# Float32 scores and output projection on TensorE: from 64x128 tiles to 64x64 tiles

## The chip, the cores and the metric

The kernel runs on one core of one Trainium2 chip. The metric is the time of one execution in device microseconds. TensorE (PE) multiplies, VectorE (DVE), ScalarE (ACT) and GpSimd (POOL) do the elementwise work, and SyncE (SP) issues the DMAs. The engines run their own programs and meet at semaphores.

## The reference

32 sequences of 256 rows with 128 channels go through a feed-forward block, an attention block and the same feed-forward block again:

```
x = x + 0.5 * ffn(layernorm(x))
x = x + attn(layernorm(x))       # linear attention: 16 heads of 8, states multiplied over K=2
x = x + 0.5 * ffn(layernorm(x))
```

The feed-forward block is a softmax attention of 16 heads of width 64, with mixtures of 8 experts at its values and at its output:

```
q, k   = x Wq[h], x Wk[h]                       # 16 heads, width 64
v      = sum_e mix[t,h,e] * (x Wv[e])           # mix: sigmoid of the two largest gates
scores = softmax(q k^T / 8)                     # 256 x 256 per head
res    = sum_h sum_e mask[t,h,e] * (attn[t,h] Wo[e])
```

All of it is float32.

## The kernel before

**Passes and quarters.** A pass is one feed-forward block of one sequence. There are 64: 7 first blocks to start with, then second and first blocks in turn (25 of each), then 7 second blocks. A pass has four quarters of four heads each, so that there are 256 quarters that attend; `n` counts quarters, and `p, r = divmod(n, 4)`. All engines run over the same quarters in a software pipeline written out by hand: in quarter n TensorE computes the scores of quarter n, the product of probabilities and values of quarter n-1, the projections q and k of quarter n+1, and transposes the probabilities of quarter n. Other passes' steps are put in at fixed quarters: the mixed values of pass p+1 at r = 2 and 3 (`values`), the output of pass p-2 at r = 1 (`output`), the expansion of the masked attention at r = 2 (`expand`), and the steps of the attention block of passes p-2 to p-4 where these were first blocks. Since first and second blocks alternate, so do two kinds of pass: I call a pass *even* where p-2 and p-4 were first blocks (passes 26 and 24, for instance, are first blocks, so pass 26 is even), and *odd* where p-3 was one.

**TensorE's order in a quarter**: scores (L373), then values (L385) at r = 2 and 3 or output (L399) at r = 1, product (L415), expand (L427) at r = 2, the projections (L432 to L434, called through `split_mm`), small steps, and 16 transposes (L453, `turn`). Each transpose group of four waits until its PSUM bank is vacant. Four banks go round in the order of the work, so that a turn waits for whatever used the bank four items before.

**Tiles of the array.** A matmul whose operands lie on 64 partitions uses half of the array's rows; one whose output has 64 partitions uses half of its columns. The trace writes rows*columns: scores and output are 64*128 (two tiles, picked by the head or by the half of the rows), values 64*64 (four tiles), product and expand 128*64 (two tiles), projections and transposes 128*128. One float32 matmul of the kernel appears as two MATMUL instructions with a weight load (PEld) each.

**Who waits for scores.** DVE takes the maxima of each pair of heads (L595), ACT takes the exponentials (L700) and then copies the next q and k from PSUM (L738). The other DVE work of a quarter follows the copy of the product (L619, which waits for the product): at r = 0 RSUM and MASKR (L598, L602, ahead of that copy), the choice of experts (`EQ`, `FW`, `MAXR`, `F`, L555 to L565) and, at r = 3, MIX (L654), which SP writes to memory and reads back as MT. POOL builds from it BT for the values (L804), and MB for expand (L810); at r = 2 of an odd pass it first normalises AA (L792 to L797) from DVE's statistics (L572, L575). At r = 2, XT is copied by ACT (L763) and DVE (L669).

Of the kernel before, what the change touches and what calls it, by code (L numbers as in the profile page):

```python
# [12 lines left out]
P = 128  # L13
# [9 lines left out]
def macaron_kernel(nc, x, WqT, WkT, WvT, WgT, WoT, aWq, aWkv, aWo, b_q, b_kv, b_o, ln_g, ln_b,  # L23
                   ident_d, diagv_d, diago_d, ramp_d, heads_d, out):
    NSEQ, T, C = x.shape
    NT = T // P
    E, DH = WoT.shape[1], WoT.shape[0]
# [6 lines left out]
    with ctx:  # L34
        def sb(name, shape, dtype=F32):
            return ctx.enter_context(nc.sbuf_tensor(name, shape, dtype))
# [18 lines left out]
        wo = sb("wo", [P, E, C])  # L55
# [17 lines left out]
        QK = sb("QK", [P, 2, 2, T])  # L73
# [33 lines left out]
        OT = sb("OT", [P, E, P])  # L107
# [17 lines left out]
        psS = ctx.enter_context(nc.psum_tensor("psS", [P, 2, 2, NT, T], F32))  # L125
# [97 lines left out]
        def bank(*item):  # L223
            return psT[:, place[item] % BANKS, :]
# [5 lines left out]
        def wait_freed(eng, *item):  # L230
            if item in place:
                eng.wait_ge(s_free[place[item] % BANKS], place[item] // BANKS + 1)

        def wait_vacant(eng, *item):

            if place[item] >= BANKS:
                eng.wait_ge(s_free[place[item] % BANKS], place[item] // BANKS)

        def full(*item):
            return s_full[place[item] % BANKS]  # L240
# [124 lines left out]
        def tensor_program(eng):  # L365
            def scores(n, ab):
                wait_freed(eng, "qk", 2 * n + ab)
                if n >= 1:
                    eng.wait_ge(s_exp, 8 * (n - 1) + 4 * ab + 4)
                for it in range(NT):  # L370
                    for j in range(2):
                        own = slice(64 * j, 64 * j + 64)
                        last = eng.matmul(psS[:, ab, j, it, :], QK[own, ab, 0, it * P:(it + 1) * P], QK[own, ab, 1, :], start=True, stop=True)  # L373
                last.then_inc(s_score)

            def values(q, half):
# [14 lines left out]
            def output(q):  # L391
                for i in range(2):
                    wait_vacant(eng, "output", q, i)
                    wait_freed(eng, "expand", q, i)
                eng.wait_ge(s_late, 16 * 14)
                for e in range(E):
                    for i in range(NT):
                        rows = slice(64 * i, 64 * i + 64)
                        last = eng.matmul(bank("output", q, i)[:, 0:C], OT[rows, e, :], wo[rows, e, :], start=e == 0, stop=e == E - 1)  # L399
                        if e == E - 1:  # L400
                            last.then_inc(full("output", q, i))

            def product(m):
                pm, r = divmod(m, 4)
# [26 lines left out]
            def split_mm(dst, left, right):  # L431
                eng.matmul(dst, left(0), right(0), start=True, stop=False)  # L432
                eng.matmul(dst, left(0), right(1), start=False, stop=False)  # L433
                return eng.matmul(dst, left(1), right(0), start=False, stop=True)  # L434
# [25 lines left out]
            for n in QUARTERS:  # L460
                p, r = divmod(n, 4)
                if works(n):
                    scores(n, 0)
                    scores(n, 1)
# [4 lines left out]
                if r == 1 and runs(p - 2):  # L469
                    output(p - 2)  # L470
# [8 lines left out]
                if r in (0, 1) and runs(p + 2):  # L479
                    q = p + 2  # L480
                    wait_vacant(eng, "expert", q, r)
                    split_mm(bank("expert", q, r), lambda c: XT[:, q % 3, c, r * P:(r + 1) * P], lambda c: wv[:, c, :]).then_inc(full("expert", q, r))
                if r == 0 and attends(p - 3):
                    q = p - 3
# [4 lines left out]
                    for k in range(2):  # L489
                        for t in range(NT):  # L490
                            last = eng.matmul(M[:, k * C:(k + 1) * C], KV[:, t, k * C:(k + 1) * C], KV[:, t, (2 + k) * C:(3 + k) * C],
                                              start=t == 0, stop=t == NT - 1)
# [3 lines left out]
                if r == 0 and attends(p - 4):  # L496
                    q = p - 4
# [5 lines left out]
                if r == 1 and attends(p - 3):  # L503
                    q = p - 3
# [6 lines left out]
                if r == 2 and runs(p + 3):  # L511
                    q = p + 3
# [4 lines left out]
                if r == 2 and attends(p - 2):  # L517
                    q = p - 2
# [3 lines left out]
                if r == 3 and runs(p + 3):  # L522
                    q = p + 3
# [4 lines left out]
                    for it in range(NT):  # L528
                        last = split_mm(M[:, it * T:(it + 1) * T], lambda c: XT[:, q % 3, c, it * P:(it + 1) * P], lambda c: wg[:, c, :])
                    last.then_inc(full("gates", q))  # L530
                if r == 3 and attends(p - 3):
                    q = p - 3
# [3 lines left out]
                if r == 3 and attends(p - 2):  # L536
                    q = p - 2
# [349 lines left out]
```

## Time and profile before

| | us |
|---|---|
| median of 3 runs | 2708.53 (2707.15 to 2710.92) |
| the profiled execution, its own time | 2715.99 |
| its span | 2714.2 |
| PE busy | 2599.0 (96%) |
| PE weight loads busy | 2310.9 (85%) |
| DVE, ACT, POOL busy | 2056.0, 1882.0, 967.4 |
| mean granted TensorE clock, share of full | 0.994 |

The ends of matmuls are modelled, and a matmul is shown longer than the time after which the next starts. So the distance between the starts of two phases says more than the busy share.

### The profile page before, as it was taken

To read this page: it belongs to the slowest core of one execution; us is meant where nothing else is said; L and a number is where in the kernel's file an instruction comes from. 1 tells how busy PE (TensorE), PEld (TensorE's weight loads), DVE (VectorE), ACT (ScalarE), POOL (GpSimd) and SP (SyncE) were. 2 spreads that over 40 slices of the span, in tenths; PEclk is the share of its full clock that TensorE was granted. 3 is DMA by queue.
4 is the path that set the end of the run, shared out by engine and by line. 5 is a ranking of instruction groups with operands and counts; after the bars stand their busy time and mean duration, and the time that the engine had idled before them with its cause. 6 is when DMAs were issued, how large, how long until landed. Compare 5 with 4: busy or idle time off the path is not lost.

```text
span 2714.2 us, 106002 instructions
## 1 busy us (share of the span) xinstructions
PE 2599.0 (96%) x43712; PEld 2310.9 (85%) x43712; DVE 2056.0 (76%) x3370; ACT 1882.0 (69%) x5957; POOL 967.4 (36%) x805
## 2 busy tenths in 40 slices
PE   4999999999999999999999999999999999999998
PEld 3888888888888888888888888888888888888897
DVE  5777777777777777777777777877777777777763
ACT  3767767677767677677777676776776766677675
POOL 2243433423424334334234243343342433433321
PEclk8999999999999999999999999999999999999998
DMA  4545445555454554555554545545555545454553
GB/s 123 158 137 144 142 134 146 140 149 148 138 153 139 139 149 144 150 142 144 149 148 138 153 135 143 147 141 153 138 144 147 148 134 145 135 155 138 145 154 101
DMA packets 519180, 387.23 MB, mean 143 GB/s; under 512 B 213936, under 2 KB 436016, under 8 KB 510512
## 3 DMA queue, kind: packets, MB, share of 16 engines
q1 hardware_dynamic: 518272, 379.60, 50.3%
q8 instruction: 352, 5.77, 0.9%
q14 instruction: 124, 1.02, 0.1%
q10 hardware_dynamic: 432, 0.85, 0.1%
HBM read 191.64 MB, written 188.74 MB: 140 GB/s over the span
## 4 chain that ended last, share of the span: by engine, by line
PE 72%; DVE 14%; ACT 8%; issue 5%; POOL 1%; DMA 0%; SPq 0%; ACTq 0%; DVEq 0%; POOLq 0%
PE psS L373 16%; PE psT L453 15%; PE psT L415 14%; PE psT L432 5%; ACT PB L700 5%; PE psT L399 4%; PE psT L434 4%; PE psT L433 4%; DVE NMAX L595 4%; PE psT L385 4%; DVE FW L559 3%; PE psT L542 2%; PE psT L427 2%; DVE EQ L555 2%; DVE AO L619 1%
## 5 line engine op out<-in xcount | busy, mean ns | idle before, releaser
L700 ACT ACTIVATE PB<-psS,NMAX 128x256 f32<-128x256 f32 x2048 | 943.5, 488 | 590.8 <-DVE NMAX L595 590.8
L595 DVE TENSOR_REDUCE NMAX<-psS 128x4 f32<-128x1024 f32 x512 | 603.1, 1220 | 102.3 <-PE psS L373 102.3
L453 PE MATMUL psT<-ident,PB 128*128 128x128 f32 x4096 | 521.5, 277 | 59.8 <-DVE XT L669 37.3
L453 PEld LDWEIGHTS psT<-ident,PB 128*128 128x128 f32 x4096 | 451.8, 141 | 127.2 <-DVE XT L669 53.3
L415 PE MATMUL psT<-V,PT 128*64 128x64 f32 x16384 | 538.2, 224 | 2.7 <-issue 2.6
L415 PEld LDWEIGHTS psT<-V,PT 128*64 128x64 f32 x16384 | 501.9, 138 | 42.1 <-issue 25.8
L373 PE MATMUL psS<-QK 64*128 64x256 f32 x4096 | 511.8, 389 | 0.0
L804 POOL TENSOR_TENSOR BT<-MT,diagv 128x1024 f32<-128x1024 f32 x128 | 320.2, 2502 | 481.4 <-DMA MT<-MIXd 481.4
L680 DVE COPY PT<-psT 128x512 f32<-128x512 f32 x512 | 353.2, 690 | 155.9 <-PE psT L453 153.8
L700 ACT ACTIVATION_READ_ACCUMULATOR PB<-psS,NMAX 128x1 f32 x2048 | 452.3, 221 | 0.0
L373 PEld LDWEIGHTS psS<-QK 64*128 64x128 f32 x4096 | 374.8, 187 | 77.4 <-issue 28.2
L619 DVE COPY AO<-psT 128x512 f32<-128x512 f32 x256 | 176.4, 689 | 289.7 <-PE psT L415 289.7
L786 ACT ACTIVATE PT<-psT 128x512 f32<-128x512 f32 x512 | 307.6, 615 | 117.4 <-PE psT L453 117.2
L738 ACT ACTIVATE QK<-psT 128x512 f32<-128x512 f32 x512 | 300.7, 629 | 45.2 <-PE psT L434 35.1
L810 POOL TENSOR_TENSOR MB<-MASKT,diago 128x1024 f32<-128x1024 f32 x128 | 247.5, 1954 | 58.2 <-DMA MASKT<-MASKd 58.2
L822 POOL TENSOR_TENSOR X<-X,bo 128x256 f32<-128x256 f32 x32 | 23.4, 730 | 635.9 <-DVE X L665 635.9
L792 POOL TENSOR_SCALAR RSTD<-MV 128x2 f32<-128x2 f32 x128 | 45.7, 357 | 534.8 <-DVE MV L575 534.7
L385 PEld LDWEIGHTS psT<-PR,BT 64*64 64x64 f32 x8192 | 132.9, 136 | 51.0 <-issue 51.0
L432 PE MATMUL psT<-XT,wq 128*128 128x256 f32 x512 | 171.7, 335 | 0.0
L385 PE MATMUL psT<-PR,BT 64*64 64x64 f32 x8192 | 150.3, 222 | 8.0 <-POOL BT L804 8.0
L708 ACT ACTIVATE VM<-psT 128x512 f32<-128x512 f32 x256 | 139.9, 612 | 9.7 <-PE psT L385 9.7
L433 PE MATMUL psT<-XT,wq 128*128 128x256 f32 x512 | 144.5, 282 | 0.0
(107 smaller groups left out, 4101.6 us busy)
## 6 DMA issues: line engine op xcount, KB each, us to landing
Vd<-VM SPq DMA_DIRECT2D x128, 512.0 KB, 3.7
V<-Vd SPq DMA_DIRECT2D x128, 512.0 KB, 4.8
AOd<-AO SPq DMA_DIRECT2D x256, 256.0 KB, 3.2
PJd<-PJ SPq DMA_DIRECT2D x64, 512.0 KB, 2.6
PR<-PJd SPq DMA_DIRECT2D x64, 512.0 KB, 4.0
MIXd<-MIX SPq DMA_DIRECT2D x64, 128.0 KB, 1.9
MT<-MIXd SPq DMA_DIRECT2D x64, 128.0 KB, 4.4
MASKd<-MASKR SPq DMA_DIRECT2D x64, 128.0 KB, 1.8
```

Source lines behind the costliest of these rows:

```text
L373: last = eng.matmul(psS[:, ab, j, it, :], QK[own, ab, 0, it * P:(it + 1) * P], QK[own, ab, 1, :], start=True, stop=True)
L385: last = eng.matmul(bank("values", q, half, a)[64 * u:64 * u + 64, k * DH:(k + 1) * DH], BT[rows, 8 * half + k, 4 * u:4 * u + 4].rearrange ...
L415: last = eng.matmul(M[64 * u:64 * u + 64, (t * NT + it) * DH:(t * NT + it + 1) * DH], PT[:, t, jt, cols], V[:, pm % 2, 4 * r + t, jt, :], ...
L432: eng.matmul(dst, left(0), right(0), start=True, stop=False)
L433: eng.matmul(dst, left(0), right(1), start=False, stop=False)
L453: last = eng.transpose(M[:, jt * T + it * P:jt * T + (it + 1) * P], PB[:, ab, j, it, jt * P:(jt + 1) * P], ident[:, :])
L595: eng.tensor_reduce(NMAX[:, ab, :, :], psS[:, ab, :, :, :], AX_X, ALU.max, negate=True).then_inc(s_max)
L680: eng.tensor_copy(PT[:, t].rearrange("p n t -> p (n t)"), bank("turn", n, t)).then_inc(freed("turn", n, t))
L700: eng.activation(PB[:, ab, j, it, :], psS[:, ab, j, it, :], ACT.Exp, bias=NMAX[:, ab, j, it:it + 1], accum_out=SUM[:, p % 2, it, head:head ...
L738: eng.activation(QK[:, ab, :, :].rearrange("p k t -> p (k t)"), bank("qk", m), ACT.Copy).then_inc(freed("qk", m))
L786: eng.activation(PT[:, t].rearrange("p n t -> p (n t)"), bank("turn", n, t), ACT.Copy).then_inc(freed("turn", n, t))
L804: eng.tensor_tensor(BT[:, 8 * half:8 * half + 8], MT[:, 4 * half:4 * half + 4, :].rearrange("p g (n h) -> p (g n) h", n=NT).unsqueeze(2).t ...
```

## The change

Each matmul of `scores` and `output` is divided into two, one for each half of the 64*128 tile's columns. The half u takes 64 columns of the weights and writes partitions 64u to 64u+63 of the same PSUM bank. The order of the four matmuls (half outside, row tile inside) is that of `values`. Nothing else is moved, and semaphores are raised by the last matmul as before.

```diff
                 for it in range(NT):
-                    for j in range(2):
-                        own = slice(64 * j, 64 * j + 64)
-                        last = eng.matmul(psS[:, ab, j, it, :], QK[own, ab, 0, it * P:(it + 1) * P], QK[own, ab, 1, :], start=True, stop=True)
+                    for u in range(2):
+                        for j in range(2):
+                            own = slice(64 * j, 64 * j + 64)
+                            low = it * P + 64 * u
+                            last = eng.matmul(psS[64 * u:64 * u + 64, ab, j, it, :], QK[own, ab, 0, low:low + 64], QK[own, ab, 1, :], start=True, stop=True)
                 last.then_inc(s_score)
...
                 for e in range(E):
-                    for i in range(NT):
-                        rows = slice(64 * i, 64 * i + 64)
-                        last = eng.matmul(bank("output", q, i)[:, 0:C], OT[rows, e, :], wo[rows, e, :], start=e == 0, stop=e == E - 1)
-                        if e == E - 1:
-                            last.then_inc(full("output", q, i))
+                    for u in range(2):
+                        for i in range(NT):
+                            rows = slice(64 * i, 64 * i + 64)
+                            cols = slice(64 * u, 64 * u + 64)
+                            last = eng.matmul(bank("output", q, i)[cols, 0:C], OT[rows, e, cols], wo[rows, e, :], start=e == 0, stop=e == E - 1)
+                            if e == E - 1 and u == 1:
+                                last.then_inc(full("output", q, i))
```

## Rows read from the trace of the kernel before

**Rows 1.** The page: span, and the chain that ended last by engine

```profile
span 2714.2 us, 106002 instructions
...
PE 72%; DVE 14%; ACT 8%; issue 5%; POOL 1%; DMA 0%; SPq 0%; ACTq 0%; DVEq 0%; POOLq 0%
```

**Rows 2.** Busy time by stretch, eight quarters: us, then each engine's

```profile
sum 83.49, PE 81.00 PEld 71.91 DVE 64.73 ACT 58.68 POOL 30.36; mean PE 10.12 PEld 8.99 DVE 8.09 ACT 7.34 POOL 3.80
```

**Rows 3.** Groups by line, all instructions of the scores: busy, mean ns

```profile
L373 PE MATMUL psS<-QK 64*128 64x256 f32 x4096 | 511.8, 389 | 0.0
```

**Rows 4.** Matmuls of one phase each: duration ns min/median/max, first and last start

```profile
L373 PE MATMUL psS<-QK x16: 376/376/480, 1150.6 to 1152.2; 64*128 64x256 f32 x16
...
L385 PE MATMUL psT<-PR,BT x64: 218/218/268, 1152.5 to 1153.5; 64*64 64x64 f32 x64
...
L399 PE MATMUL psT<-wo,OT x32: 269/272/272, 1142.7 to 1144.3; 64*128 64x128 f32 x32
...
L415 PE MATMUL psT<-V,PT x64: 222/222/270, 1153.6 to 1155.5; 128*64 128x64 f32 x64
```

**Rows 5.** Timeline of PE in pass 26, r = 1 and 2: start us, length us

```profile
1140.82 2.00 PE L373 MATMUL psS<-QK 64*128 64x256 f32 x16
1142.65 1.95 PE L399 MATMUL psT<-wo,OT 64*128 64x128 f32 x32
1144.53 2.08 PE L415 MATMUL psT<-V,PT 128*64 128x64 f32 x64
...
1150.61 2.00 PE L373 MATMUL psS<-QK 64*128 64x256 f32 x16
1152.54 1.16 PE L385 MATMUL psT<-PR,BT 64*64 64x64 f32 x64
1153.63 2.08 PE L415 MATMUL psT<-V,PT 128*64 128x64 f32 x64
```

**Rows 6.** Timeline of pass 25 (odd), r = 2, which starts at 1110.13

```profile
1110.57 3.86 POOL L810 TENSOR_TENSOR MB<-MASKT,diago 128x1024 f32<-128x1024 f32 x2
...
1113.98 0.30 DVE L575 BATCH_NORM_AGGREGATE MV<-STAT 128x2 f32<-128x6 f32 x2
1114.45 0.23 POOL L792 TENSOR_SCALAR RSTD<-MV 128x2 f32<-128x2 f32 x1
...
1115.41 0.69 DVE L619 COPY AO<-psT 128x512 f32<-128x512 f32 x1 [1.13 <-PE psT L415]
...
1117.13 2.53 POOL L804 TENSOR_TENSOR BT<-MT,diagv 128x1024 f32<-128x1024 f32 x1
1117.45 2.49 DVE L559 TENSOR_TENSOR FW<-EQ,rampb 128x512 bf16<-128x512 bf16 x1
...
1121.78 0.66 PE L453 MATMUL psT<-ident,PB 128*128 128x128 f32 x4 [1.39 <-DVE XT L669]
```

**Rows 7.** Timeline of pass 21 (odd), r = 2, which starts at 944.43

```profile
951.43 2.46 POOL L804 TENSOR_TENSOR BT<-MT,diagv 128x1024 f32<-128x1024 f32 x1
951.68 2.49 DVE L559 TENSOR_TENSOR FW<-EQ,rampb 128x512 bf16<-128x512 bf16 x1
```

**Rows 8.** Timeline of pass 26 (even), r = 2, which starts at 1150.61

```profile
1158.66 1.31 ACT L738 ACTIVATE QK<-psT 128x512 f32<-128x512 f32 x2
...
1159.06 0.28 PE L434 MATMUL psT<-XT,wk 128*128 128x256 f32 x1
```

**Rows 9.** Timeline of pass 25 (odd), r = 3, which starts at 1122.36

```profile
1129.36 1.15 ACT L738 ACTIVATE QK<-psT 128x512 f32<-128x512 f32 x2
...
1130.07 1.85 PEld L453 LDWEIGHTS psT<-ident,PB 128*128 128x128 f32 x16 [0.28 <-ACT QK L738]
```

**Rows 10.** Timeline of pass 27 (odd), r = 0, which starts at 1172.60

```profile
1176.02 2.39 POOL L804 TENSOR_TENSOR BT<-MT,diagv 128x1024 f32<-128x1024 f32 x1 [14.05 <-DMA MT<-MIXd]
...
1176.43 2.26 DVE L602 TENSOR_TENSOR MASKR<-MASK,RSUM 128x256 f32<-128x256 bf16 x1
...
1182.37 0.66 PE L453 MATMUL psT<-ident,PB 128*128 128x128 f32 x4 [0.56 <-DVE ST L661]
```

## The prediction

> **What bounds the kernel now.** I read the page first: the chain that ended last is 72% TensorE, 14% DVE, 8% ACT [rows 1]. Then the busy time by stretch: in eight quarters of 83.49 us TensorE is busy for 81.00 [rows 2]. So TensorE mostly sets the pace, but what I have to know is in which quarters it waits, and for a chain that begins where. For that I read the timelines of two neighbouring passes, one even and one odd, and looked for the wait that ends last in each quarter. The quarters repeat from pass to pass within some tens of ns, apart from single gaps of about 0.1 us.
>
> **What a phase costs.** Scores: 16 instructions, 2.00 us from first start to last end [rows 5]. The last lasts 376 ns, so it starts at 1.624. The first lasts 480 against 376: 104 ns of weight load that nothing hides, as it follows a change of tile shape [rows 4]. The two tiles start some 7 ns apart, so the eight rounds of two follow each other every (1.624 - 0.104 - 0.007) / 7 = 216 ns. Values, four tiles: 1.16 - 0.218 = 0.942 to the last start, 50 ns of it exposed load (268 against 218); product, two tiles of the same 64 columns: 2.08 - 0.222 = 1.858, with 48 exposed. Two equations, 15 rounds + 3 staggers = 0.892 and 31 rounds + 1 stagger = 1.810, give a round of 58 ns for both and a stagger of 6 to 7 ns. So four tiles run in the time of two. A switch costs more than the load: from the last start of scores to the next phase 1.93 - 1.624 = 306 ns, which is a round and 90 ns of drain; from scores to output, same shape, 1.83 - 1.624 = 206, less than a round, no drain, and the first matmul of output (269) shows no exposed load [rows 4, 5]. From values to product: 1.09 - 0.942 = 148, a round and 90 again. The drain counts from the last tile.
>
> **The scores after.** 32 instructions in eight rounds of four, each streaming 256 columns: 8 x 216 as before. The first load is of 64 columns: 50 ns instead of 104, since four tiles enter values with 50. Two more staggers add 13. The last start comes at 1.624 - 0.054 + 0.013 = 1.583, 41 ns earlier, and the last of the first pair of heads is earlier by the same 41. No row shows 64*64 tiles with 256 columns. Bounds: a load of 104 again (then 13 ns worse, not 41 better) and an exposed load of nothing (91 better); I take 50, which both 64-column shapes show. Entry from the transposes: the drain of 90, as at the other switches.
>
> **What follows them.** At r = 0 product: 41 ns earlier. At r = 1 output: no switch before or after; it starts at 8 rounds + 0.050 = 1.778 instead of 1.83 and has 16 rounds as before, its two staggers come back at the end, so product starts 40 ns earlier. At r = 2 and 3 values: scores and values now share a shape. Values start at 1.778 instead of 1.93 (152 ns), and their own 50 ns load lies under the last round, as output's does now: 0.20 us in all. Bounds here: nothing hidden and the drain kept (0.04), or all of it (0.20); output's row is the nearest, I take 0.20. If TensorE bound every quarter, a pass would gain 40 + 40 + 200 + 200 = 480 ns, 64 passes 31 us.
>
> **Where the gain does not arrive.** DVE's maxima start when scores end, so every chain that begins with them gains only the 41 ns.
> - Odd, r = 2: TensorE waits 1.39 us for XT, which is behind `FW` on DVE. `FW` took 2.49 us; it ends 0.28 after BT ends on POOL (1117.13 + 2.53 = 1119.66; 1117.45 + 2.49 = 1119.94) [rows 6]. While a POOL tensor_tensor runs, this bf16 operation is held. BT's start is set by POOL's chain from L792, and that by the statistics (end 1114.28, start 0.17 later) and by MB's end (1114.43) at nearly the same time. The statistics move by 41 ns, MB not, so L792 by about 30. Product's 200 only make `FW` queue longer. Gain 30 ns.
> - Odd, r = 3: the transposes start at 1130.07, when ACT's first copy of QK ends; ACT works without a gap from exponentials through QK, GS and AAT [rows 9]. Gain 41 ns.
> - Odd, r = 0: MASKR takes 2.26 us and ends 0.28 after BT (1178.41, 1178.69); the wait at 1182.37 follows from it through copies, choice of experts and ST [rows 10]. BT waited for MT by DMA, which SP reads back only after MIX of the quarter before is written. MIX comes 0.20 earlier, as AO and the product before it do, but so does the end of that quarter. Measured from its own start, this quarter gains nothing.
> - Even, r = 2: here ACT's second copy of QK waits for the projection (L434 ends at 1159.06 + 0.28 = 1159.34, the copy runs from about 1159.37), and behind it come XT and a transpose that waits for XT [rows 8]. Two copies without a wait take 1.15 us [rows 9], these take 1.31. So ACT could start the second 0.16 earlier now and, being 0.04 earlier itself, 0.20 earlier then: just as much as the projection moves. I take 0.20, and nothing is left over.
> - Even, r = 3: TensorE runs through to the last transpose: 0.20. Even r = 0: ACT's copies end last: 0.04. Both r = 1: 0.04.
>
> **The sum.** Even pass: 0.04 + 0.04 + 0.20 + 0.20 = 0.48. Odd: 0 + 0.04 + 0.03 + 0.04 = 0.11. 25 of each: 14.8 us. Of the 14 passes at the two ends, the first seven behave like even ones (about 3), the last seven gain about half (1.7). Sum 19.5 us: the profiled execution goes from 2716.0 to 2696.5. It stands 7.5 above the median of the runs, so for the median I say 2708.5 - 19.5 = 2689.
>
> **A rule against it.** The scores now want 32 instructions in 1.6 us, twice as many as before, and 4096 + 2048 more pairs in all; the nearest row is values, 64 in 0.94 us, 15 ns each, so the sequencer has three times the rate needed [rows 4, 5]. The Trainium skill (TensorE: Matmul & The Clock Gate, section "Wait — 56ns, not 53.3ns?") says that with hardware decoding off the sequencer spends about 62 ns per MATMUL; by that, as an estimate from the page, scores would last 32 x 62 = 1.98 us, 0.34 longer than I say to the last start, and the kernel would be some 70 us slower. The values contradict it here.
>
> **Rivals.**
> 1. *TensorE binds after all*, the waits of odd passes follow it: 31 us, 2678. Against it stand the waits of three quarters [rows 6, 9, 10]. Chance 6%.
> 2. *`FW` starts before BT.* It starts 0.32 after BT, and comes 0.17 nearer (0.20 less 0.03). In pass 21 it starts only 0.25 after BT, as it does in eight of the odd passes [rows 7]: there 0.08 us are left, and less if DVE was held up a little by BT already. If `FW` starts first, BT waits for it (0.5 us), and `F` is what is held, up to about 1120.1 + 0.5 = 1120.6, where it now ends at 1119.94 + 0.04 + 0.69 + 0.03 + 0.69 = 1121.4: 0.8 us per pass. In 8 to 25 passes: 6 to 20 us more, 2669 to 2683. Chance 10%.
> 3. *The change saves no time*: load and drain stay at the entry to values, four tiles enter scores with 104 ns. Then 13 ns a quarter are lost, 256 x 0.013 = 3 us: 2712. The phases before show both otherwise [rows 4, 5]. Chance 4%.
> 4. *Slower: rounds of two.* A float32 matmul is two instructions on one tile (4096 for 2048 calls) [rows 3]. They run four abreast in values only if those of four calls are interleaved. If here only pairs were, the second instruction of one pair would run beside the first of the next, and the scores would take nine rounds instead of eight, output 17 instead of 16: 216 ns more in every quarter and 112 at r = 1. Against gains of 0.04 to 0.20, and with the chains of odd passes moved too, that is some +0.6 us a pass, 2745. It decides as soon as a quarter has one extra round. The order of calls is that of values, which speaks against it. Chance 5%.
> 5. *Slower by issue rate.* 8 x 216 / 32 = 54 ns per instruction is what the scores allow; if each took 64, 32 x 10 ns = 0.3 us a quarter would be lost, 82 us in all against the 20, 2770. It decides from 54 ns on; values run at 15. Chance 1%. Of other waits that I did not see (BT late for values, MB late for expand, single gaps) I say: 1% slower than 0.2%, 3% within it.
>
> **How the numbers follow.** The forecast has 70%, its own range 2682 to 2697: the ends are even quarters at r = 2 stopped by ACT (25 x 0.1 less) or an exposed load off by 20 ns, and up to four odd passes of rival 2. Faster by over 0.2% (5.4 us, about what a measurement here can tell): 70 + 6 + 10 = 86%. Within: 4 + 3 = 7%. Slower: 5 + 1 + 1 = 7%. The range runs from 2671, which takes in rivals 1 and most of 2, to 2698.
>
> **What the profile after would show.** Scores as 64*64 x8192 with min 376 and max about 426; output x4096 with about 272; scores' start to product's start 1.89 at r = 0; to values' start 1.78 and values' longest matmul 218; even quarters at r = 2 and 3 0.20 shorter, odd ones 0.03 to 0.04, odd r = 0 unchanged. `FW` in odd passes still near 2.5 us, or longer; if it drops to 0.5, rival 2 holds. A round of scores of more than 216 ns, or nine rounds, would make the prediction wrong.

## The result

The kernel after the change takes 2770.11 us (median of 5 runs, 2765.07 to 2777.89) against 2708.53 for the kernel before in the same job (2704.68 to 2715.46): ratio 1.0229, 95% interval 1.0203 to 1.0254. I had forecast 2689, in a range of 2671 to 2698. The sign is wrong, and the time is off by 81 us.

The page of the kernel after: span, busy time, the DMA queue of instructions, the chain that ended last, and four groups by line (busy us, mean ns of one, idle before it and its releaser).

```profile
span 2776.1 us, 118290 instructions
...
PE 2592.6 (93%) x49856; PEld 2252.6 (81%) x49856; DVE 2066.4 (74%) x3370; ACT 1883.4 (68%) x5957; POOL 956.9 (34%) x805
...
q8 instruction: 400, 6.55, 1.1%
...
L419 PE MATMUL psT<-V,PT 128*64 128x64 f32 x16384 | 563.5, 226 | 57.9 <-issue 56.6
...
L419 PEld LDWEIGHTS psT<-V,PT 128*64 128x64 f32 x16384 | 518.6, 140 | 112.1 <-issue 102.8
...
L375 PE MATMUL psS<-QK 64*64 64x256 f32 x8192 | 501.2, 382 | 0.0
```

TensorE is *less* busy than before (2592.6 against 2599.0 us), and the scores cost 501.2 us where they cost 511.8 [rows 3]: both as the change promises. The new item stands at product (probabilities times values), L419, a line that the change doesn't touch: 56.6 us of idle time that ends with "issue", no engine and no semaphore. The waits of TensorE (us in total, times, longest), after and then before, show how new that is.

```profile
PE psT L419 <- issue: 56.6, 58, 3.3
PE psT L457 <- DVE XT L673: 53.8, 48, 1.6
...
PE psT L403 <- issue: 1.8, 1, 1.8
PE psT L387 <- issue: 1.0, 1, 1.0
```

```profile
PE psT L453 <- DVE XT L669: 37.3, 27, 1.5
...
PE psT L415 <- issue: 2.6, 6, 0.7
```

**The phases are as predicted.** Scores, output, values and product in pass 26, r = 1 and 2, first as durations (min/median/max), then as timeline (start, length):

```profile
L375 PE MATMUL psS<-QK x64: 376/376/427, 1165.0 to 1176.3; 64*64 64x256 f32 x64
...
L387 PE MATMUL psT<-PR,BT x64: 216/218/218, 1176.5 to 1177.4; 64*64 64x64 f32 x64
...
L403 PE MATMUL psT<-wo,OT x64: 269/269/269, 1166.7 to 1168.4; 64*64 64x128 f32 x64
```

```profile
1174.69 1.96 PE L375 MATMUL psS<-QK 64*64 64x256 f32 x32
1176.46 1.11 PE L387 MATMUL psT<-PR,BT 64*64 64x64 f32 x64
1177.51 0.57 PE L419 MATMUL psT<-V,PT 128*64 128x64 f32 x12
1178.37 1.74 PE L419 MATMUL psT<-V,PT 128*64 128x64 f32 x52 [0.29 <-issue]
```

Scores to values takes 1176.46 - 1174.69 = 1.77 us (forecast 1.78, before 1.93 [rows 5]); the exposed load is 427 - 376 = 51 ns (forecast 50), and values' longest matmul is 218: no switch. Values to product is 1.05 instead of 1.09. Then comes the line that I had not foreseen: product stops after 12 of 64 matmuls, for 0.29 us by this view (0.51 between two starts; matmul ends are modelled), in the middle of a phase whose operands are all there.

**A long one.** Pass 20, r = 1. Product gets 15 matmuls out and then stands for 2.75 us. The timeline of TensorE, with SP's issue of the load of AR:

```profile
908.00 0.82 SPq L353 DMA_DIRECT2D AR<-AOd  x1
...
909.40 1.96 PE L375 MATMUL psS<-QK 64*64 64x256 f32 x32
...
911.18 1.93 PE L403 MATMUL psT<-wo,OT 64*64 64x128 f32 x64
...
913.04 0.68 PE L419 MATMUL psT<-V,PT 128*64 128x64 f32 x15
...
916.47 2.40 PE L419 MATMUL psT<-V,PT 128*64 128x64 f32 x49 [2.75 <-issue]
```

And the DMA queues in the stretches 906 to 910, 910 to 913.5 and 913.5 to 916.5 (busy tenths of the DMA engines in 40 slices; packets, MB, share):

```profile
DMA  9620003899999600000014867899999984219929
...
q1 hardware_dynamic: 2294, 0.48, 66.7%
```

```profile
DMA  2348249899999999999986599989999999969997
...
q1 hardware_dynamic: 482, 0.99, 94.6%
```

```profile
DMA  9979999531000000000010101100000000000000
...
q1 hardware_dynamic: 179, 0.17, 22.6%
q8 instruction: 1, 0.02, 2.5%
```

Queue 8 carries the instructions of TensorE's program: 400 packets for 6.55 MB, so 16.4 KB each, 256 instructions of 64 bytes (before the change 352 packets, 5.77 MB). No packet of it falls between 906 and 913.5 us. There loads fill the DMA engines (94.6%), that of AR, issued at 908.00 and landing 6.5 us later, first of all; the next packet starts at 913.8, ends at 915.0, and 1.45 us later product goes on. TensorE had run out of instructions.

**All stops are at one place of the stream.** I numbered the records of TensorE's queue from 0, semaphore instructions included. All 66 stops over 0.12 us in a product end at number 193 or 194 of every 256 (a matmul; its weight load is 192 or 193), and 1.2 to 1.6 us after a packet of queue 8 has landed. The same holds for all 603 such stops in products of the 18 profiles of this case. The numbering begins with the first record of the profile, so it doesn't say where in it a piece begins; below, "border" means this fixed place. The stops of product in passes 16 and 20, r = 1, are 6400 = 25 x 256 records apart; the view by stretches has 3116 matmuls and 3116 loads from the one to the other, and the other 168 are semaphore instructions:

```profile
746.30:916.46 170.16, 161.45 (x3116) 140.50 (x3116) 128.40 (x210) 117.51 (x372) 60.58 (x50) 0.99 0.52 141
```

An even and an odd pass together now have 3200 instructions on TensorE, 12.5 pieces; before they had 2816, 11 pieces. So the borders fall on the same matmuls every four passes, and the stops recur there.

The Trainium skill (Runtime: NRT & Kernel Launch, section "Instruction fetch mechanics") says that an engine's program is streamed in blocks of 16 KiB, 256 instructions, over a DMA queue of the sequencer; the sizes here agree. It also says that the cost of crossing a block is "mostly hidden". For most of the 400 pieces that is so here, but 60 waits, 59.4 us in all, are not hidden.

**The clock follows.** Stretches of 3.4 us around the long stop (the last three numbers are granted clock, DMA share and GB/s):

```profile
912.80:916.20 3.40, 0.92 (x27) 0.61 (x20) 0.61 (x3) 2.77 (x13) 0.00 (x0) 1.00 0.44 114
916.20:919.60 3.40, 3.13 (x52) 3.01 (x52) 0.69 (x2) 0.00 (x0) 0.00 (x0) 0.62 0.02 5
919.60:923.00 3.40, 3.40 (x25) 3.22 (x25) 2.66 (x11) 2.27 (x4) 1.85 (x3) 0.88 0.22 80
```

After 3 us without matmuls the granted clock of TensorE falls from 1.00 to half (0.62 and 0.88 are mixtures), 2.4 to 1.2 GHz, for 3.4 us. The 49 matmuls after the stop take 2.40 us, where 52 took 1.74 in the quarter above. With its stop this quarter is 14.17 us long, and that of pass 22 (r = 1, no stop) 9.71: 4.5 us for a stop of 2.98 between two starts.

**Where the 62 us lie.** I took the distances between the starts of scores of neighbouring quarters, after less before, for quarters 32 to 231, 25 of each kind:

| us | even | odd |
|---|---|---|
| r = 0 | -0.5 | -3.9 |
| r = 1 | **+45.6** | -0.7 |
| r = 2 | **+21.6** | -9.0 |
| r = 3 | -4.3 | -0.1 |

With +8.0 before and +3.5 behind them it is 60.2. Even r = 1 is up to 0.08 us shorter where it has no stop (10 of 25), and up to 4.6 longer where it has one. At even r = 2 something else is added to a short stop. The timeline of DVE and POOL in pass 26, whose product stopped for 0.5 us:

```profile
1182.19 0.56 DVE L563 TENSOR_TENSOR FW<-EQ,rampb 128x512 bf16<-128x512 bf16 x1
...
1182.78 0.69 DVE L565 TENSOR_REDUCE MAXR<-FW 128x64 bf16<-128x512 bf16 x1
...
1182.80 2.37 POOL L808 TENSOR_TENSOR BT<-MT,diagv 128x1024 f32<-128x1024 f32 x1
...
1183.50 2.21 DVE L569 TENSOR_TENSOR F<-FW,MAXR 128x512 bf16<-128x512 bf16 x1
```

DVE's chain begins with product and comes late; POOL's doesn't. So BT now starts before `F`, and `F` takes 2.21 instead of 0.69 us; XT and the transpose behind it wait (1.17 us). `F` is held like this in 18 of the 25 even passes, and `FW` in one more. Nine of the 18 have a stop of 0.29 us or more in their own product. Six others follow a stop of 1.9 us or more at r = 1, and POOL's RSTD comes 4.6 to 5.0 us into the quarter instead of 5.3. The other three had 0.13 us or less; why they are held is not shown. In odd passes it went the other way, as my rival 2 had it: in 13 of 25 `FW` starts before BT and takes 0.42 us, and `F` is the one held. Those are the 13 whose product doesn't stop; in the other 12 it stops for 0.12 to 0.41 us, and `FW` is held as before. Pass 23:

```profile
1056.52 0.42 DVE L563 TENSOR_TENSOR FW<-EQ,rampb 128x512 bf16<-128x512 bf16 x1
...
1056.97 2.37 POOL L808 TENSOR_TENSOR BT<-MT,diagv 128x1024 f32<-128x1024 f32 x1
...
1057.70 2.18 DVE L569 TENSOR_TENSOR F<-FW,MAXR 128x512 bf16<-128x512 bf16 x1
```

### The profile page after: what moved, and what is told of

It reads as the page before. It is cut to its first block, busy times and chain, and to the rows that moved or that the text cites. A ratio compares the mean times of both kernels' runs of the same rounds, so it can differ in the third digit from the quotient of the medians.

```text
span 2776.1 us, 118290 instructions
## 1 busy us (share of the span) xinstructions
PE 2592.6 (93%) x49856; PEld 2252.6 (81%) x49856; DVE 2066.4 (74%) x3370; ACT 1883.4 (68%) x5957; POOL 956.9 (34%) x805
## 3 DMA queue, kind: packets, MB, share of 16 engines
q8 instruction: 400, 6.55, 1.1%
## 4 chain that ended last, share of the span: by engine, by line
PE 77%; DVE 11%; issue 5%; ACT 4%; POOL 1%; DMA 1%; SPq 0%; DVEq 0%; ACTq 0%; POOLq 0%
PE psT L419 17%; PE psS L375 16%; PE psT L457 15%; PE psT L436 6%; PE psT L438 5%; PE psT L437 5%; PE psT L403 4%; PE psT L387 4%; ACT PB L704 3%; DVE NMAX L599 2%; PE psT L431 2%; PE psT L546 2%; DVE EQ L559 2%; DVE FW L563 2%; DVE MAXR L565 1%
## 5 line engine op out<-in xcount | busy, mean ns | idle before, releaser
L419 PE MATMUL psT<-V,PT 128*64 128x64 f32 x16384 | 563.5, 226 | 57.9 <-issue 56.6
L419 PEld LDWEIGHTS psT<-V,PT 128*64 128x64 f32 x16384 | 518.6, 140 | 112.1 <-issue 102.8
L457 PE MATMUL psT<-ident,PB 128*128 128x128 f32 x4096 | 520.1, 277 | 73.8 <-DVE XT L673 53.8
L375 PE MATMUL psS<-QK 64*64 64x256 f32 x8192 | 501.2, 382 | 0.0
L808 POOL TENSOR_TENSOR BT<-MT,diagv 128x1024 f32<-128x1024 f32 x128 | 310.5, 2426 | 550.5 <-DMA MT<-MIXd 550.5
L375 PEld LDWEIGHTS psS<-QK 64*64 64x64 f32 x8192 | 288.0, 132 | 139.5 <-issue 28.2
L387 PEld LDWEIGHTS psT<-PR,BT 64*64 64x64 f32 x8192 | 144.9, 136 | 27.5 <-issue 12.4
L387 PE MATMUL psT<-PR,BT 64*64 64x64 f32 x8192 | 144.5, 220 | 8.7 <-POOL BT L808 7.7
```

The lines of the kernel that those rows point to most:

```text
L375: last = eng.matmul(psS[64 * u:64 * u + 64, ab, j, it, :], QK[own, ab, 0, low:low + 64], QK[own, ab, 1, :], start=True, stop=True)
L387: last = eng.matmul(bank("values", q, half, a)[64 * u:64 * u + 64, k * DH:(k + 1) * DH], BT[rows, 8 * half + k, 4 * u:4 * u + 4].rearrange ...
L419: last = eng.matmul(M[64 * u:64 * u + 64, (t * NT + it) * DH:(t * NT + it + 1) * DH], PT[:, t, jt, cols], V[:, pm % 2, 4 * r + t, jt, :], ...
L457: last = eng.transpose(M[:, jt * T + it * P:jt * T + (it + 1) * P], PB[:, ab, j, it, jt * P:(jt + 1) * P], ident[:, :])
L808: eng.tensor_tensor(BT[:, 8 * half:8 * half + 8], MT[:, 4 * half:4 * half + 4, :].rearrange("p g (n h) -> p (g n) h", n=NT).unsqueeze(2).t ...
```

## The experiments

**The theories.** F: TensorE's instruction stream, 256 instructions at a time, comes too late where the work before a border is dense; the added instructions make it denser and move the borders. Against it stand S (the shape of the tiles, or the matmul at which it stops), B (the changed order on DVE and POOL is the cause) and T (issue of matmuls or their PSUM writes); each expectation says what its rival would give. "Waits for issue" is the sum of those in TensorE's list of waits, for the profiled execution: 2.6 us before, 59.4 after.

**1 and 2. Each part alone.** The diff of `scores` alone, and that of `output` alone.

> The changed kernel with output put back to 64x128 tiles (scores stay in 64x64): 4096 matmul instructions more than before instead of 6144. Theory F (fetch): TensorE's own instruction stream arrives in pieces of 16 KB (256 instructions), and the matmuls stall where a piece is late; the cost grows with instructions per microsecond. Then most of the 3 us stalls of product at r = 1 become shorter, since r = 1 has 64 instructions less ahead of product, those at r = 2 stay (some 12 us); 2715 to 2745, stalls of product 20 to 50 us against 73. Theory S (shape): the 64x64 tiles of scores, with 256 columns, are themselves what slows the next phase. Then all of it stays: 2765 to 2775.

Measured: 2719.38 us, ratio 1.0007 (0.9991 to 1.0022), waits for issue 20.4.

> Output in 64x64 tiles, scores put back: 2048 matmul instructions more than before, all at r = 1. F: stalls at r = 1 only, 15 to 35 us; output saves nothing itself and now switches shape after scores (+0.15 us in 62 quarters, 9 us): 2725 to 2750. S: no stalls in product, 2717.

Measured: 2739.12, ratio 1.0092 (1.0075 to 1.011), waits for issue 20.6. Both times lie in F's ranges; product's own waits with scores alone, 18.9 us, are just under the 20 forecast. Each part makes stops, at places of its own: scores alone at r = 3 and 2, output alone at even r = 1 (+20.1 us there). With scores alone odd r = 2 gains 16.6 us (`FW` before BT) and both r = 1 lose about 0.17 us a quarter, since output now follows a phase of another shape. The parts don't add up to the whole (0.07% and 0.9% against 2.3%), as a cost per instruction would.

**3. The same number of instructions in the old shape.** Scores stay 64*128 and are halved in the columns that they stream.

```diff
-                    for j in range(2):
-                        own = slice(64 * j, 64 * j + 64)
-                        last = eng.matmul(psS[:, ab, j, it, :], QK[own, ab, 0, it * P:(it + 1) * P], QK[own, ab, 1, :], start=True, stop=True)
+                    for v in range(2):
+                        for j in range(2):
+                            own = slice(64 * j, 64 * j + 64)
+                            part = slice(P * v, P * v + P)
+                            last = eng.matmul(psS[:, ab, j, it, part], QK[own, ab, 0, it * P:(it + 1) * P], QK[own, ab, 1, part], start=True, stop=True)
```

> The kernel before with each scores matmul divided along the moving side (2 x 128 columns) in the old 64x128 tiles: the instruction count of e1, no change of tile shape. By the rounds of output (112 ns for 128 columns) the scores take 16 x 112 instead of 8 x 216, 60 ns more a quarter, 15 us. F: stalls like those of e1 on top, 20 to 50 us: 2740 to 2775. S: no stalls: 2720 to 2727.

Measured: 2722.87, ratio 1.0033 (1.0022 to 1.0044). Theory F as I had put it missed, and the time lies in the range of S: the same 384 packets as in experiment 1, at the same borders, and 1.8 us of waits for issue instead of 20.4. What differs is time: scores' start to values' start is 1.99 us here and 1.78 there. So the number alone doesn't make a stop; by F it takes the number in the time since the last piece. That the 64*64 shape itself does it (S) was not excluded by this run.

**4. Moving what fills the DMA engines.** The kernel after; SP issues the load of AR at the end of r = 1 instead of the end of r = 0.

```diff
-                if r == 0 and runs(p - 1):
+                if r == 1 and runs(p - 1):
                     q = p - 1
...
```

> The changed kernel with one DMA issue moved: AR<-AOd (1 MB in packets of 512 B, 6.6 us to landing) goes from the end of r = 0 to the end of r = 1 on SP's queue; expand needs it only at r = 2. F: the late fetches at r = 1 wait behind this load, so the long stalls (2 to 3.5 us, 40 us in all) go, though some may come back around r = 2, where the load now runs: 2720 to 2750. S, or a stall that has nothing to do with DMA: 2765 to 2775 as the changed kernel.

Measured: 2748.67, ratio 1.012 (1.0093 to 1.0147). The list of TensorE's waits:

```profile
PE psT L421 <- issue: 61.7, 52, 2.3
PE psT L433 <- issue: 22.0, 25, 1.5
...
PE psT L389 <- issue: 0.2, 1, 0.2
```

The stops at r = 1 are gone (40.1 us before the edit, 0.1 now, by the distances between starts), and even r = 1 is 0.08 us *shorter* than in the kernel before. New ones of up to 2.3 us stand at r = 2, where the load now lies: in even passes in product and in expand (L433), in odd ones mostly in product. Not one instruction of TensorE was changed. This speaks for F and against S. The sum of the waits for issue rose, though, from 59.4 to 83.9 us, while the time fell by 21 (2770.1 to 2748.7): TensorE waits 12.3 us for XT instead of 53.8. So what a stop costs depends on what else waits there. (In the trace, the load of AR is 512 packets of 2 KB, not of the 512 B that I had expected.)

**5 to 7. Moving the borders.** 40 or 104 more instructions (pairs of satisfied waits) once at TensorE's start, so that every border falls that much earlier in the same work: on scores alone (5 and 6) and on the kernel before (7).

```diff
+            for _ in range(2 * 40):
+                eng.wait_ge(s_const, 80)
             for n in QUARTERS:
```

> The kernel with only the scores in 64x64 tiles (2719 us), and once, ahead of all work of TensorE, 80 waits on a semaphore value that is long reached, which are 40 instructions. No work is added in the loop. Theory F: what counts is where the borders of the 256-instruction pieces fall. In the trace of that kernel the stalls come at the same two or three places of each pair of passes; shifting the borders by 40 instructions puts them where 256 instructions last longer. Counting on that trace with a latency of 3.4 us from about 230 instructions ahead, the stalls fall from 32 to about 5 us: 2688 to 2702. Without F, 40 waits at the start can't change anything: 2719 within 3.

Measured: 2744.01, ratio 1.013 (1.0111 to 1.015), waits for issue 27.9 in a profile of 2732.4 us span.

> The same with 104 instructions at the start instead of 40. F: the borders fall inside product behind values, where 256 instructions pass in 3 us; by the same count stalls of 75 us instead of 32: 2750 to 2775. Without F: 2719 within 5.

Measured: 2772.88, ratio 1.0232 (1.0214 to 1.0251), waits for issue 64.5, of which 21.0 is one wait at the start; first scores start only 1.2 us later than without.

> The kernel before, unchanged but for the same 40 instructions at the start. F: the kernel before owes its few stalls (6 us) to the place of its borders (2816 = 11 x 256 instructions in a pair of passes); shifted by 40, stalls of 30 to 50 us: 2740 to 2755. Without F: 2709 to 2719, no change.

Measured: 2706.02, ratio 0.9982 (0.9973 to 0.9992), waits for issue 2.2. Two of the three forecasts missed: I had a rule for which border would be late, and it was wrong; experiment 7 lies below the ranges of both theories. But 40 and 104 instructions at the start, of some 98,000, made the same kernel 25 and 54 us slower, with its stops at other matmuls (with 104, also in values: 9.9 us). With 40, the profiled execution is only 14 us longer than that of experiment 1, and odd r = 2 alone is 16.6 longer there: its gain is gone again (`FW` is held in 23 passes instead of 5, and 17 of these quarters have a stop instead of 5). So those 40 act through the order of `FW` and BT more than by the length of the stops. Nothing in S explains that. The kernel before has slack at its borders, and stays.

**8. Taking away the hold of `FW`.** Of the kernel before: BT half 1 waits for `F` of its quarter.

```diff
                 if r == 2 and runs(p + 1):
+                    if runs(p + 2):
+                        eng.wait_ge(s_pick, PICKS * (p + 2) + 11)
                     spread_mix(p + 1, 1)
```

> The kernel before, where POOL starts BT of r = 2 only after DVE's F (one more wait, POOL's instruction only). Theory L: a POOL tensor_tensor that runs holds up a bf16 tensor_tensor of DVE until it ends, so who comes first decides over 1 to 2 us on DVE's chain to XT. Then FW in odd passes takes 0.45 instead of 2.49 us, and r = 2 of odd passes gets shorter by 1.0 to 1.4 us: 25 to 35 us in all, 2680 to 2692. If FW is long for another reason: no gain, 2709 to 2719.

Measured: 2681.41, ratio 0.9893 (0.9878 to 0.9908). DVE in pass 25, r = 2, and BT:

```profile
1107.05 0.43 DVE L559 TENSOR_TENSOR FW<-EQ,rampb 128x512 bf16<-128x512 bf16 x1
1107.51 0.69 DVE L561 TENSOR_REDUCE MAXR<-FW 128x64 bf16<-128x512 bf16 x1
1108.23 0.69 DVE L565 TENSOR_TENSOR F<-FW,MAXR 128x512 bf16<-128x512 bf16 x1
```

```profile
1109.01 2.37 POOL L804 TENSOR_TENSOR BT<-MT,diagv 128x1024 f32<-128x1024 f32 x1 [2.18 <-DVE F L565]
```

`FW` takes 0.43 instead of 2.49 us [rows 6], nothing else is held, and odd r = 2 is 1.5 us shorter. And a side effect: 13.5 us of waits for issue in product, mostly at odd r = 3, in a kernel with TensorE's old program. Running faster is enough to make the stream late.

**9. The kernel after, with the same wait.**

> The kernel after, with one wait more on GpSimd: BT half 1 at r = 2 starts only when F of DVE is done (s_pick at 11 of its 18 marks), so that neither FW nor F can be held by it, whatever TensorE does. Theory F (TensorE's instruction stream comes late at 256-instruction borders): the stalls inside product stay, about 60 to 80 us of them; what goes is the 2.2 us F in 19 of 25 even quarters at r = 2 (up to 21 us) and the same hold in odd ones (about 30 us). 2705 to 2745. Theory B (the loss is the changed order of BT and F on DVE and GpSimd, and the gaps of TensorE only follow from it): the gaps go too, and the time is below the kernel before with the same wait (2681), by about the 20 us of the prediction: 2655 to 2680.

Measured: 2738.25, ratio 1.0096 (1.0075 to 1.0117). TensorE's waits:

```profile
PE psT L419 <- issue: 73.6, 79, 2.5
...
PE psT L403 <- issue: 1.8, 1, 1.8
...
PE psT L457 <- DVE XT L673: 0.4, 1, 0.4
```

F held, B fell: with no hold left on DVE (XT 0.4 us instead of 53.8) the stops are more, not fewer. Against experiment 8, the same kernel with the old scores and output, it is 57 us slower with 62.3 us more of waits for issue (76.0 against 13.7). The loss of the change is the stops; the holds cost both kernels about the same, 32 us here (2770.1 to 2738.3) and 30 there (2711.7 in that job to 2681.4). Less their waits for issue the two stand at 2662 and 2668, with the low clock of the longer stops (mean granted clock 0.987 against 0.996) still in the first.

**10. Experiment 8 with 40 more instructions at the start.**

> The kernel before with BT after F (2681 in the batch before, with 18 us of stalls in product at r = 3) and 40 more instructions once at TensorE's start, so that every border of 256 falls 40 instructions earlier in the work. Theory F: the stalls at r = 3 go or move; 2660 to 2680 if they go, up to 2700 if they fall into values or product at r = 2; no stall stays at the same matmul. Theory S (the stall at r = 3 belongs to that matmul's operands or bank): nothing changes, 2678 to 2686.

Measured: 2675.28, ratio 0.9865 (0.9849 to 0.9881), waits for issue 13.0 (19 stops over 0.12 us instead of 28). The time is inside what F gives, and the waits hardly fell. But the stops moved, and that decides against S. Product in pass 47, r = 3, in experiment 8 and then here:

```profile
2013.76 1.15 PE L415 MATMUL psT<-V,PT 128*64 128x64 f32 x32
2015.65 1.15 PE L415 MATMUL psT<-V,PT 128*64 128x64 f32 x32 [0.74 <-issue]
```

```profile
2008.48 0.57 PE L415 MATMUL psT<-V,PT 128*64 128x64 f32 x12
2009.61 1.74 PE L415 MATMUL psT<-V,PT 128*64 128x64 f32 x52 [0.56 <-issue]
```

Of the stops at odd r = 3, 23 of experiment 8 come after 32 matmuls of product, and 14 here after 12: 20 matmuls with their 20 weight loads are the 40 instructions. The same shift is in experiments 1 and 5 (even r = 3: after 37, then 17). A stop belongs to a place of the instruction stream and not to a matmul, its operands, its shape or its PSUM bank. And both kernels have TensorE's old tiles.

**11. The number of instructions alone, by filling.** The kernel before with 4 satisfied waits' instructions behind each matmul of scores and output.

> The kernel before, every matmul as it was, with 4 more instructions (satisfied waits) behind each matmul of scores and output, so that TensorE's program has the same number of instructions as the kernel after (102,411 against 102,410 by its size) in the same phases. It computes what the kernel before does. Theory F: the number of instructions and their density is the cause, so stalls of 1 us and more appear in product at every few borders, 40 to 110 us in all, 2735 to 2800. Theory T (64x64 tiles with 256 columns, or their writes to PSUM, are the cause, or the issue of matmuls as such): the waits lie in the sequencer's slack, 2705 to 2725.

Measured: 3524.25, ratio 1.2996 (1.2974 to 1.3018). Not a test of what I wanted: the 12,288 instructions added cost 806 us of span, 66 ns each (two waits in each; the mean granted clock was 0.918), where a matmul with its load takes 15 in values. So theory T was not tested by it. It shows one thing on the side. The queue of instructions has the same 400 packets as after the change, and product waits for issue 0.7 us in all: in a program that runs slower, as many pieces are never late.

**12. A better kernel.** Experiment 8, and BT half 0 waits for MASKR, which it had held for 2.26 us [rows 10].

```diff
                 if r == 1 and runs(p + 1):
+                    if runs(p - 1):
+                        eng.wait_ge(s_maskr, p)
                     spread_mix(p + 1, 0)
```

> The kernel before with BT half 1 after F (2681 in the batch before) and BT half 0 after MASKR too (GpSimd waits for s_maskr). MASKR then takes about 0.5 us instead of 2.26 in odd quarters at r = 0, and the choice of experts behind it comes earlier. If the wait for ST at 1182.37 (0.56 us) follows from it, odd quarters at r = 0 gain up to 0.56 us, 25 x 0.5 = 12 us: 2665 to 2675. If BT half 0, which comes 1 to 2 us later, holds another operation of DVE instead, or values wait for it, no gain: 2680 to 2695.

Measured: 2668.70, ratio 0.9842 (0.9821 to 0.9862), the fastest kernel here, 43 us below the one before in that job. Pass 27, r = 0:

```profile
1160.66 0.42 DVE L602 TENSOR_TENSOR MASKR<-MASK,RSUM 128x256 f32<-128x256 bf16 x1
...
1161.16 2.38 POOL L804 TENSOR_TENSOR BT<-MT,diagv 128x1024 f32<-128x1024 f32 x1 [14.63 <-DVE MASKR L602]
```

**13 to 16. Is the predicted gain there at all?** Experiment 12 with scores in 64*64 tiles, with 0, 168 and 216 more instructions at the start; and experiment 12 itself with 40.

> Scores in 64x64 tiles, output as before, BT half 1 after F and BT half 0 after MASKR (that base alone took 2669). Gain of the steps: scores to values without a switch 0.20 us at r = 2 and 3, 0.04 at r = 0, and about 0.16 us lost at r = 1 where output now follows another shape; 50 quarters of each kind, some 14 us if all of it arrives. Theory F: plus stalls that depend on where the borders fall, 30 us of them on the base without these waits; 2665 to 2695. No gain at any place: 2669 plus the stalls.

Measured: 2692.21, ratio 0.992 (0.9903 to 0.9936).

> The same with 168 more instructions once at TensorE's start. The instructions after that and their order are the same. Theory F: the amount of stalls changes by tens of us with the place of the borders, and so does the time: 2650 to 2720, different from the run without them by over 10 us. Were the place of no weight, the time would be the same within 3 us.

Measured: 2713.85, ratio 0.9998 (0.9988 to 1.0007).

> The same with 216 more. As for 168: another place of the borders, another amount of stalls, 2650 to 2720; I have no rule that says which place is best, and the waits for issue in product plus the stall-free time should make up each of the three times within 5 us.

Measured: 2682.93, ratio 0.988 (0.9865 to 0.9894).

> The base of these (scores and output as before, BT half 1 after F and BT half 0 after MASKR) with 40 more instructions at the start. With 40 the base without the wait for MASKR went from 2681 to 2675. 2658 to 2669 under F, with about as much in waits for issue as there (13 us).

Measured: 2672.22, ratio 0.9839 (0.9824 to 0.9854): no gain from 40, 3 us outside the forecast; waits for issue 8.2.

The added instructions cost time at the start, which I had left out: the first scores start at 60.2 and 67.4 us with 168 and 216, at 53.0 with none, so 7.2 and 14.4 us of the two times are the padding itself. Less padding and less the other waits for issue the three stand at 2654, 2655 and 2649 us, within 6 of each other where I had said 5. Experiment 12 less its 13.6 us of waits stands at 2655 as well, and each of the three takes longer than it: no kernel here is faster for the change, and its gain shows only quarter by quarter. The distance from first to last scores against experiment 12 is +21.3, +40.2 and +1.3 us: one program, three places of its borders. By kind of quarter (difference to experiment 12, quarters 32 to 231, median in ns):

| | exp. 13 | exp. 14 | exp. 15 |
|---|---|---|---|
| even r = 0 | -18 | **+840** | -18 |
| even r = 1 | +178 | **+1048** | +177 |
| even r = 2 | -123 | -128 | -129 |
| odd r = 2 | -131 | -131 | -131 |
| even r = 3 | **+572** | -200 | -33 |

The bold entries are where stops are that experiment 12 doesn't have, in experiment 14 in the projections too (L434, 26.9 us, a phase of large matmuls, with the old tiles: neither S nor T has a reason for it). Odd r = 3 isn't in the table, since experiment 12 itself has 11.8 us of stops there (18.5, none and 14.3 in the three). Outside the bold entries nearly the same value comes back: 18 and 130 ns gained, and 0.17 lost at r = 1, where output has the old shape; 200 gained at even r = 3, once whole, and 33 in experiment 15, which has nine small stops there. That is the change at work, free of its side effect. (With output too, r = 1 gains 0.08: 0.43 us for an even pass, about 0.25 for an odd one, 17 us in 25 of each, where I had 14.8. This is a sum over quarters; no run shows it as a time.)

## Why the prediction was wrong

**The step that failed** is the one under "A rule against it", and with it rival 5: the added matmuls and loads were costed at nothing because TensorE issues one such pair every 15 ns in values. That is true, and issue was not the limit. What I did not price is that 12,288 more instructions are 48 more pieces of 256 to bring in by DMA, and that the denser phases leave less time for each. Scores, values, product and expand at r = 2 are 448 instructions in 6.7 us now (without a stop), 416 in 6.9 before: 3.8 us per piece instead of 4.2. The shortest distance between the starts of two packets in the trace is 3.4 us, and at the stops 2.2 to 2.9 us lie between the start of the packet and the next matmul. That leaves 0.4 us, and the load of AR takes more than that. These are means over a phase: the densest 256 records in a row take 2.9 us in either kernel, so density at one place doesn't decide by itself. The sign was there before the change, in TensorE's list of waits: six waits of product for issue, 2.6 us, all at the same place of the stream. The chain's "issue" share didn't tell, since it is 5% before [rows 1] and after. Rival 5's 2770 us is the measured time by chance: it stands on 64 ns an instruction, and the round of scores is still 216 ns.

**What held.** A round of 216 ns, the exposed load of 50, the last start of scores 40 ns earlier (1.582 after the first, against 1.583 forecast), product at r = 0 after 1.89, no switch into values, and 0.20 for even r = 3 (0.200 measured). The small ones were off by as little as they are: 0.04 at r = 1 was 0.08, 0.04 at even r = 0 and odd r = 3 was 0.02. Odd r = 0, put at nothing, came 3.9 us shorter in sum; it is 3.1 shorter in experiment 3 as well, whose tiles are the old ones, so the new shape isn't needed for it, and I did not follow it up. Rivals 3, 4 and the issue rate of rival 5 did not happen.

**Even r = 2** was forecast 0.20 shorter, and is 0.12 to 0.13 where nothing is held (experiments 13 to 15); ACT probably gives less than I let it (in the kernel after, TensorE's transposes wait for its copy of QK 17 times instead of 5). A size, worth 2 us. In the kernel after it is 0.87 longer: stop and held `F`.

**Odd r = 2** was forecast 0.03 shorter with `FW` still held. Rival 2 came true in 13 of 25 passes, at 0.78 us each (it said 0.8), in each one whose product didn't stop. It had 10%, since I had worked out 0.08 us left before BT. That was no margin: in pass 21 `FW` now starts 7.05 us into the quarter, BT starts at 6.98 where it is first, and yet it was `FW` that went first, with BT at 7.50. POOL's operation before BT took 1.31 us there instead of 0.80. So more than the two start times decides the order. Odd r = 2 came 9 us shorter in sum.

**The sum** would have been 2716 - 19.5 for the steps and about -9 for rival 2, near 2687; the stops, their low clock and the `F` that they expose turn it into 2776.

**What stays open.** Which border will be late: I tried to foretell it and missed twice in three. The pieces, their time in the DMA engines and the one place of every 256 records are read from traces; the rule by which a packet is asked for is not, and I did not find why a packet starts when it does. That the 64*64 shape as such plays no part rests on experiments 4 to 6, 8, 10 and 13 to 15 together, where stops move without it or stand in kernels that have the old tiles; a program with as many matmuls in the same time in another shape was not built. How much of the 62 us is the stops themselves and how much the holds behind them is known only roughly (experiments 4 and 9).

## What to carry to other kernels

When a change divides matmuls on an engine that is nearly always busy, count its instructions in pieces of 256 and the time that the dense phases give for a piece, and look at what else the DMA engines carry there; a gain of 40 to 200 ns a phase is soon paid back by one late piece of a few tenths to 3 us, plus the low clock behind it. A wait whose releaser is "issue" inside a phase with its operands ready is the sign to look for, at a line that the change never touched. And before moving any work by tens of ns, remove the holds that depend on who starts first: two waits on POOL were worth 43 us here, twice the 19.5 that I had forecast for the change.

## What the runs showed of the hardware that I had not expected

- TensorE's program is brought in by DMA in pieces of 256 instructions (16.4 KB, 0.9 to 1.9 us each in flight). A late piece stops the engine for up to 3.3 us, at the same place of every 256 records (all 603 stops over 0.12 us in products, in 18 profiles), 76 us in all in experiment 9.
- The same program is 25 or 54 us slower by where its borders fall (experiments 5 and 6, in part through what the stops do to DVE's order), and a kernel made faster elsewhere can begin to stop (experiment 8: 2.6 to 13.7 us).
- While loads fill the DMA engines (94.6% busy, 0.99 MB in 3.5 us) the piece doesn't come; moving the issue of one load moves the stops (experiment 4).
- A bf16 tensor_tensor of DVE that meets a tensor_tensor of POOL lasts to about its end: 2.49, 2.21 or 2.18 us instead of 0.43 or 0.69; a reduction between them isn't held (0.69 us with BT running).
- An instruction of two satisfied waits costs TensorE's queue some 66 ns between matmuls (experiment 11, part of it low clock) and 150 at the start (7.2 us for the 48 more of experiment 15 against 14), against 15 for a matmul with its load in values.
